# Fused attention stage: transposed scores beside the scores, and maxima subtracted in PSUM by TensorE

## What is computed

```python
def _L1_xattn_ref(query, key, value, ...):
    qn = _layer_norm(query, ln1_g, ln1_b)
    kn = _layer_norm(key, ln1_g, ln1_b)
    vn = _layer_norm(value, ln1_g, ln1_b)
    Q = (qn @ wq + bq).reshape(B, Sq, H, HD)
    K = (kn @ wk + bk).reshape(B, Sk, H, HD)
    V = (vn @ wv + bv).reshape(B, Sk, H, HD)
    scores = jnp.einsum('bqhd,bkhd->bhqk', Q, K) / jnp.sqrt(jnp.float32(HD))
    attn = jax.nn.softmax(scores, axis=-1)
    out = jnp.einsum('bhqk,bkhd->bqhd', attn, V).reshape(B, Sq, E)
    x = residual + out @ wo + bo
    y = _layer_norm(x, ln2_g, ln2_b)
    return x + jax.nn.gelu(y @ w1 + b1, approximate=False) @ w2 + b2
```

## Time and profile of the kernel before

| | |
|---|---|
| median of 3 runs | 1391.83 us (1389.43 to 1393.59) |
| profiled execution, its own time | 1399.14 us |
| span of its trace | 1397.3 us |
| granted TensorE clock, mean | 0.967 of 2.4 GHz |
| busy: TensorE, VectorE, ScalarE, GpSimd | 89%, 68%, 71%, 64% |
| fused stage with its projections | about 916 to 1264 us of the span |
| last feed-forward | about 1264 to 1397 us |

### The profile page before, as it was taken

One profiled execution on the slowest core, in us unless ns is written; L12 is line 12 of the kernel. 1 busy time (PEld: TensorE's weight loads), 2 busy tenths in 40 slices (PEclk: granted clock), 3 DMA queues, 4 the chain that ended last, 5 costly groups with the idle time before them and its releaser, 6 DMA issues. The chain is left out here.

```text
span 1397.3 us, 59862 instructions
## 1 busy us (share of the span) xinstructions
PE 1242.1 (89%) x23050; PEld 1031.0 (74%) x23050; DVE 953.1 (68%) x2152; ACT 988.4 (71%) x1972; POOL 899.7 (64%) x1432
## 2 busy tenths in 40 slices
PE   4999999989999998958999999985878788788997
PEld 2777877777878887837999999953666666665775
DVE  3888888876787886594555555546889999854331
ACT  1778777767888887346787776624988888865553
POOL 2577777776677665216999998767677777413331
PEclk9999999999999999579999999997999999999999
DMA  4233343322222220051222222243222222112221
GB/s 125 77 108 117 110 126 106 114 86 86 83 82 83 82 76 26 16 136 39 69 65 68 66 67 67 66 143 103 63 68 68 73 73 73 41 49 61 68 74 39
DMA packets 137984, 109.81 MB, mean 79 GB/s; under 512 B 16928, under 2 KB 113696, under 8 KB 137888
## 3 DMA queue, kind: packets, MB, share of 16 engines
q1 hardware_dynamic: 129440, 91.22, 22.1%
q0 software_dynamic: 8448, 17.32, 5.2%
HBM read 74.35 MB, written 34.08 MB: 78 GB/s over the span
## 5 line engine op out<-in xcount | busy, mean ns | idle before, releaser
L907 DVE TENSOR_REDUCE at_mx<-at_ps_s 128x16 f32<-128x1024 f32 x128 | 156.0, 1220 | 91.9 <-PE at_ps_s L587 47.2
L813 ACT ACTIVATE at_pt<-at_ps_t 128x1024 f32<-128x1024 f32 x128 | 130.6, 1020 | 55.3 <-PE at_ps_t L608 54.5
L2357 POOL DMA_INDIRECT ex_xg<-x,ex_ti x136 | 146.3, 1076 | 23.5 <-issue 21.9
L806 ACT ACTIVATE at_pr<-at_dd 128x1024 f32<-128x1024 f32 x128 | 135.2, 1056 | 34.7 <-DVE at_dd L915 34.6
L2471 DVE COPY ex_wt<-experts 128x1156 f32 x133 | 102.7, 772 | 80.4 <-DVE ex_y L2477 74.4
L2429 ACT ACTIVATE ex_hg<-ex_ps_h,ex_wt 128x128 f32<-128x128 f32 x544 | 154.6, 374 | 1.2 <-PE ex_ps_y L2388 1.2
L915 DVE TENSOR_TENSOR at_dd<-at_ps_s,at_mx 128x1024 f32<-128x1024 f32 x128 | 153.7, 1202 | 0.1
L2379 PE MATMUL ex_ps_h<-ex_xt,ex_wt 128*128 128x128 f32 x1088 | 146.5, 278 | 1.0 <-ACT ex_xt L2421 0.8
L2016 POOL DMA_INDIRECT l_yg<-rows,l_sl x128 | 125.8, 983 | 31.9 <-issue 29.4
L608 PE MATMUL at_ps_t<-ident,at_pr 128*128 128x128 f32 x1024 | 140.0, 280 | 6.0 <-issue 5.4
L2388 PE MATMUL ex_ps_y<-ex_wt,ex_hg 128*128 128x128 f32 x1088 | 143.6, 275 | 0.4 <-ACT ex_hg L2429 0.4
(11 more groups left out here) (264 smaller groups left out, 3166.5 us busy)
## 6 DMA issues: line engine op xcount, KB each, us to landing
rows<-ex_y SPq DMA_DIRECT2D x136, 64.0 KB
x<-at_ln_out SPq DMA_DIRECT2D x32, 256.0 KB, 3.2
at_kx<-in_xt SPq DMA_DIRECT2D x16, 256.0 KB, 2.8
at_qx<-in_xt SPq DMA_DIRECT2D x16, 256.0 KB, 2.8
at_vin<-in_xt SPq DMA_DIRECT2D x16, 256.0 KB, 2.8
at_xr<-in_x SPq DMA_DIRECT2D x16, 256.0 KB, 3.0
cx<-in_ctx SPq DMA_DIRECT2D x16, 256.0 KB, 3.2
x1t<-at_xt SPq DMA_DIRECT2D x16, 256.0 KB, 3.3
```

Source lines behind the costliest of these rows:

```text
L806: act.activation(pr[:, p], dd[:, p], ACT.Exp, scale=SCALE).then_inc(p_ready, 1)
L813: act.activation(pt[:, 2 * h + p], ps_t[:, :, :, :], ACT.Copy).then_inc(pt_ready, 1)
L907: dve.tensor_reduce(mx[:, p], ps_s[:, :, 4 * p:4 * p + 4, :], AX.X, ALU.max).then_inc(mx_ready, 1)
L2357: pool.indirect_dma_start(out=xg[:, s, :], out_offset=None, in_=x_src, in_offset=bass.IndirectOffsetOnAxis(ap=ti[:, s:s + 1], axis=0)).the ...
```

## The change

Scores are now made in units i = 0 to 3 of a group (half h = i // 2, row-group pair rp = i % 2) of two row groups with all four sequences. `scores(a, i)` makes the unit's products and, in between, the transposed products of the unit before, with K as the moving and Q as the stationary operand exchanged, straight into `ps_t`. VectorE takes the maxima of the untransposed unit and splits each into three parts, of which the upper 16 bits are bf16 numbers (`split`, two subtractions of 128x16). TensorE turns these parts with one bf16 product (`turn_largest`), ScalarE copies them (`copy_largest`), and TensorE subtracts them from the transposed scores by 8 bf16 products into the same PSUM tile (`take_largest`). ScalarE then takes the exponential from PSUM into `pt`. `subtract`, `turn`, `copy_t` and the buffers `dd` and `pr` are gone. K is masked by 8 DMAs a half from SyncE (SBUF to SBUF) instead of by ScalarE; its bias is added when it is projected. The Q mask and the copy of V are split by halves. Half of V is staged in `x3` instead of in `dd` and `pr`, and the last stage uses `pt` for its late buffers. `project_out` waits for one more semaphore (`y_ready`), and the steps of all five engines are written in another order. The diff of the core; the lists of `step` are shown for VectorE and GpSimd:

```diff
+                def mask_k(a, h):
+
+                    if a.unrolled and a.g == 0 and h == 0:
+                        sp.wait_ge(kt_ready, NG)
+                        sp.wait_ge(set_up, 2)
                     if beyond(a.g, 0):
+                        sp.wait_ge(s_ready, 4 * a.g + 2 * h - 1)
+                    for j in range(2):
+                        for r in range(4):
+                            heads = slice(32 * r + 16 * j, 32 * r + 16 * j + 16)
+                            sp.dma_start(kb[heads, h, :, j, :],
+                                         zt[heads, bass.ds(a.place * GT + GT // 2 * h, GT // 2)].rearrange(
+                                             "p (b s) -> p b s", b=QB)).then_inc(in_k[h], 16)
...
+                def scores(a, i):
+
+                    n, h, rp = 4 * a.g + i, i // 2, i % 2
+                    before_h = h if rp == 1 else 1 - h
+                    own, last = a.exists(), i > 0 or a.shift(-1).exists()
+                    if own and rp == 0:
+                        pe.wait_ge(in_k[h], 16 * 8 * (a.g + 1))
+                        pe.wait_ge(qb_ready[h], a.g + 1)
+                    if own and beyond(n, 0):
+                        pe.wait_ge(mx_ready, n)
+                    elif own:
                         pe.wait_ge(kt_ready, NG)
                         pe.wait_ge(vt_ready, NG)
+                    if last and beyond(n, 2):
+                        pe.wait_ge(pt_ready, n - 2)
                     for b in range(QB):
+                        if own:
+                            for r in range(2):
+                                rows = slice(64 * rp + 32 * r, 64 * rp + 32 * r + 32)
+                                mm = pe.matmul(ps_s[:, r, 2 * b:2 * b + 2, :], qb[rows, h, b, :, :], kb[rows, h, b, :, :],
+                                               start=(b == 0), stop=(b == QB - 1), skip_group_check=True)
+                        if last:
+                            for r in range(2):
+                                rows = slice(64 - 64 * rp + 32 * r, 64 - 64 * rp + 32 * r + 32)
+                                mm = pe.matmul(ps_t[:, 1 - rp, r, b, :], kb[rows, before_h, b, :, :],
+                                               qb[rows, before_h, b, :, :], start=(b == 0), stop=False,
+                                               skip_group_check=True)
                     mm.then_inc(s_ready, 1)
+                def turn_largest(a, i):
+
+                    n, rp = 4 * a.g + i, i % 2
+                    pe.wait_ge(parts_ready, n + 1)
+                    if beyond(n, 0):
+                        pe.wait_ge(pt_ready, n)
+                    pe.matmul(ps_t[:, 1 - rp, 0, 0, :], mx[:, rp, :].bitcast(BF16).rearrange("p (x t) -> p x t", t=2)[:, :, 1],
+                              same_b[:, :], start=True, stop=True).then_inc(mt_ready, 1)
+
+                def take_largest(a, i):
+
+                    n, rp = 4 * a.g + i, i % 2
+                    pe.wait_ge(mc_ready, n + 1)
+                    for b in range(QB):
+                        for r in range(2):
+                            rows = slice(64 * rp + 32 * r, 64 * rp + 32 * r + 32)
+                            mm = pe.matmul(ps_t[:, rp, r, b, :], minus[rows, b, :], mt[rows, :], start=False,
+                                           stop=(b == QB - 1), skip_group_check=True)
+                    mm.then_inc(t_ready, 1)
...
+                def exponent(a, i):
+                    n, h, rp = 4 * a.g + i, i // 2, i % 2
+                    if a.unrolled and n == 0:
+                        act.wait_ge(v_out, 16 * NG)
+                    act.wait_ge(t_ready, n + 1)
+                    if beyond(a.g, 0):
+                        act.wait_ge(pv_ready, 2 * a.g + h - 1)
+                    act.activation(pt[:, h, :, 2 * rp:2 * rp + 2, :].rearrange("p b r q -> p r b q"), ps_t[:, rp],
+                                   ACT.Exp, scale=SCALE).then_inc(pt_ready, 1)
+                def copy_largest(a, i):
+                    n, rp = 4 * a.g + i, i % 2
+                    half = slice(64 * rp, 64 * rp + 64)
+                    act.wait_ge(mt_ready, n + 1)
+                    if beyond(n, 1):
+                        act.wait_ge(t_ready, n - 1)
+                    act.activation(mt[half, :], ps_t[half, 1 - rp, 0, 0, :], ACT.Copy).then_inc(mc_ready, 1)
...
+                def maximum(a, i):
+                    n, rp = 4 * a.g + i, i % 2
+                    dve.wait_ge(s_ready, n + 1)
+                    if beyond(n, 1):
+                        dve.wait_ge(mt_ready, n - 1)
+                    dve.tensor_reduce(largest(rp, 0), ps_s[:, :, :, :], AX.X, ALU.max).then_inc(mx_ready, 1)
+                def split(a, i):
+                    n, rp = 4 * a.g + i, i % 2
+                    dve.wait_ge(mx_ready, n + 1)
+                    dve.tensor_tensor(largest(rp, 1), largest(rp, 0), high(rp, 0), ALU.subtract).then_inc(rest_ready, 1)
+                    dve.wait_ge(rest_ready, n + 1)
+                    dve.tensor_tensor(largest(rp, 2), largest(rp, 1), high(rp, 1), ALU.subtract).then_inc(parts_ready, 1)
...
+                    if a.shift(-1).exists():
+                        recip(g * 2 - 2, 0)
                     if a.exists():
-                        subtract(g * 2 + 1, 0)
+                        maximum(a, 0)
+                        split(a, 0)
                     if a.shift(3).exists():
                         weigh_first(a.shift(3))
+                    if a.shift(-1).exists():
+                        normalise(a.shift(-1), 0)
                     if a.exists():
-                        maximum(g * 2 + 1, 1)
+                        maximum(a, 1)
+                        split(a, 1)
+                    if a.shift(-2).exists():
+                        residual(a.shift(-2))
+                    if a.shift(3).exists():
+                        weigh_second(a.shift(3))
                     if a.shift(-1).exists():
                         recip(g * 2 - 1, 1)
-                    if a.shift(3).exists():
-                        weigh_second(a.shift(3))
                     if a.exists():
-                        subtract(g * 2 + 1, 1)
+                        maximum(a, 2)
+                        split(a, 2)
                     if a.shift(3).exists():
                         own_statistics(a.shift(3))
                     if a.shift(-1).exists():
                         normalise(a.shift(-1), 1)
+                    if a.unrolled and -3 <= g < -1:
+                        for e in ((5, 6, 7, 8), (11, 12, 13, 14, 15))[g + 3]:
+                            keep_v(e)
+                    if a.shift(2).exists():
+                        gain_own(a.shift(2))
+                    if a.exists():
+                        maximum(a, 3)
+                        split(a, 3)
                     if a.shift(2).exists():
                         next_statistics(a.shift(2))
                     if a.shift(3).exists() or a.shift(2).exists():
                         front_moments(a.shift(3))
-                    if a.unrolled and -3 <= g < -1:
-                        for e in ((5, 6, 7, 8), (11, 12, 13, 14, 15))[g + 3]:
-                            keep_v(e)
-                    if a.unrolled and g == -1:
-                        dve.wait_ge(v_out, 16 * NG)
-                    if a.shift(1).exists():
-                        maximum(g * 2 + 2, 0)
-                        maximum(g * 2 + 2, 1)
-                        subtract(g * 2 + 2, 0)
-                        subtract(g * 2 + 2, 1)
-                    if a.exists():
-                        recip(g * 2, 0)
-                    if a.shift(3).exists():
-                        gain_own(a.shift(3))
-                    if a.shift(-1).exists():
-                        residual(a.shift(-1))
-                    if a.shift(1).exists():
-                        maximum(g * 2 + 3, 0)
-                    if a.exists():
-                        normalise(a, 0)
...
+                    if a.unrolled and g == 0:
+                        pool.wait_ge(v_out, 16 * NG)
+                    if a.shift(-1).exists():
+                        spread(g * 2 - 2, 0)
                     if a.shift(2).exists() or a.shift(1).exists():
                         front_rstd(a.shift(2))
                     if a.shift(3).exists():
-                        fetch(a.shift(3), 5, 6)
-                        fetch(a.shift(3), 6, 7)
-                        fetch(a.shift(3), 7, 8)
-                    if a.shift(-1).exists():
-                        spread(g * 2 - 2, 0)
+                        fetch(a.shift(3), 5, 8)
                     if a.shift(4).exists():
                         fetch_open(a.shift(4))
                     if a.shift(-1).exists():
                         add_bias(a.shift(-1))
-                    if a.shift(4).exists():
-                        fetch(a.shift(4), 0, 1)
-                        fetch(a.shift(4), 1, 2)
-                        fetch(a.shift(4), 2, 3)
```

(31 more changed lines are left out.)

245 lines of the change are left out of this document (115 added, 130 removed).

## The result

The changed kernel takes **1484.93 us** (median of 4 runs, 1481.51 to 1488.6) beside 1392.28 us of the kernel before: ratio 1.0669, 95% interval 1.0638 to 1.07. That is 93 us more; 1459 was forecast, in a range of 1424 to 1486, so the measured time lies 1 us inside the upper end. The profiled execution took 1488.6 us with a span of 1486.8 us, 89.5 us longer than the span of before. (The two profiled executions stand 4 and 7 us above the medians of their kernels, which is why 89.5 and 93 differ.)

What follows compares the result with a forecast made beforehand. VectorE was taken to set the pace, busy 92 of 100 us, the other engines close behind. Profiled 1399.1 us + 71 for twelve longer steps - 4 outside them = 1466, as a median 1459 us; range 1424 to 1486.

Steps and rivals of the forecast that it cites:

- The ring: Steps 1 to 12: spread, late gathers, `weigh_first`, `values`, `gain_own`, `shift_own`, next spread; 24.0 us a step for 18.07, +71 us.
- The clock: TensorE's pause ahead of `values` drops the clock to half in all twelve steps; `values` takes 3.6 us instead of 2.0.
- Rival 1: Twelve steps: the ring without the clock drop, step 22.4 us, +48 us, 1440 us in all; chance 0.27.
- Outside the twelve steps ... -4 us: Steps 13 to 15 gain 1 us each, the start 1 us; VectorE's set-up 0 to +3 us, last stage 0.
- rival 3: K's DMAs end last as well in the twelve steps: +1.5 us a step, +18 us, 1477 us; chance 0.12.
- K by DMA, cost 0: Sixteen DMAs a step replace ScalarE's K maskings, hidden by the gather wait: cost 0, bound +1.5 us a step.
- late next: K's DMAs in the steps: were the gather wait that hides them gone, they would be the next to come late.
- The small operations on VectorE: Eight new operations on 128x16 a step, 0.2 us each, 1.6 us together, within 0 to 4.3 us.
- Rival 2: Gathers arrive without holding VectorE: step about 17.0 us, -17 us, 1375 us in all; chance 0.09.
- rival 4: Whole kernel: nothing moves, the waits given up and made cancel, 1392 us; chance 0.03.
- The step without the ring, "some 17 us": Steady step if only the engines' work changed and nothing else happened: falls from 18.07 to some 17 us.

Runs made afterwards that it cites:

- gathers_early: Changed kernel with gathers 5 to 7 of a group issued a step earlier, in the same step as its gathers 0 to 4; 1427.59 us.
- weigh_later: Changed kernel with `weigh_first` moved on VectorE behind `normalise` and `residual`, directly ahead of `weigh_second`, gathers still late; 1443.74 us.
- start_order: Changed kernel with VectorE's second group of `keep_v` moved behind the statistics and moments in two steps ahead of the first; 1472.77 us.
- orders: `early_take_start` with `recip` moved ahead of `weigh_second` on VectorE and `copy_v(a,0)` behind the exponent of unit 3 on ScalarE; 1422.05 us.
- k_on_dve: Changed kernel with K masked by products on VectorE instead of by SyncE's sixteen DMAs a step; 1483.89 us.
- early_take_start: Changed kernel with gathers as in `gathers_early`, start as in `start_order`, and `take_largest` of units 0 and 2 ahead of `values`; 1422.11 us.

## Why the prediction was right, and where it was off

- **The ring.** Right, by term and in sum: 24.0 us forecast, 23.99 measured. Spread to first gather 3.1 us (3.18 forecast), three gathers 3.57 (3.57), landing 1.77 (1.57), `weigh_first` and `normalise` 1.5 (1.58), `values` 3.6 (3.6), from its end to the end of `gain_own` 5.2 (5.4), `shift_own` and three gathers 4.9 (5.0). `gathers_early` and `weigh_later`, which open it at two different places, take 59 and 40 us back. That the sum is right to 0.01 us is in part luck: small errors of 0.1 to 0.2 us cancel, and the second path through `values(a,0)`, which I did not look at, happened to end 0.05 us ahead of the ring.
- **The clock.** The mechanism was right (0.50 under `values` in all five steps looked at, 0.86 over 100 us); its size, 1.6 us a step, was too large. Held, it gave 0.8 to 1.05, although `values` did fall to 2.0 us; the other 0.6 us are the wait of the first spread for its reciprocal, by the second path. Rival 1's step of 22.4 us would have been 22.9.
- **"Outside the twelve steps ... -4 us".** This term was mis-sized: measured +18.5 (12.0 ahead, 2 in steps 13 and 14, 4.5 behind the last load). I costed VectorE's set-up and looked no further at the start; the change had also swapped `keep_v` with the front work there, whose price `start_order` gives as 12 us. And I gave steps 13 to 15 a gain of 1 us each for freed engines; steps 13 and 14 lost 1 us each instead (18.1 us beside 17.1). TensorE was not freed there, and `orders` gets 17.2 with `recip` and `copy_v` in other places. The 4.5 us at the end were not tried by themselves; that the last stage costs 0 was nearly right (0.8).
- **The number.** With the ring exact, the term above alone puts the forecast 22.5 us low in the span. That 1484.93 still lies under 1486 is luck: the upper end was placed above rival 3 (1477), whose mechanism did not come, and no term of the range allowed for 18.5 us outside the twelve steps.
- **K by DMA, cost 0.** Right, by the one wait of 0.7 us in 160 and by `k_on_dve`. The pitch was 0.73 us, near the upper of my two ends; "late next" is what `orders` shows.
- **The small operations on VectorE.** 0.2 us each was forecast; 0.17 us alone, 0.2 on average in the changed kernel, up to 1.9 us beside GpSimd's addition in `orders`.
- **Rivals.** Rival 2, gathers that hold nobody, is excluded by the 6.1 us wait of `weigh_first`; rival 3, K's DMAs on the path, by TensorE's single wait for them and by `k_on_dve`; rival 4 by the time.
- **The step without the ring, "some 17 us".** Too low: 20.2 with early gathers (at a clock of 0.95 to 0.97), 19.1 at best. 17.2 is reached only where there is no front work, and the old form takes 17.1 there.

## What to carry to other kernels

When a change reorders hand-written queues, look at what each wait holds up behind it: here a wait for gathers placed ahead of one small multiplication made one loop through all four engines, and the step 5.9 us longer in spite of the work saved. Opening that loop gave back 3.8 of the 5.9: when the largest wait goes, the next path is often close behind, so look for it before you price the repair. Read the unrolled steps at the ends with the same care as the loop; two swapped calls cost 12 us there. And before relieving two engines, ask whether the third, which gets their work, is not the one that sets the pace once the slack is gone.

## What the runs showed of the hardware

A VectorE subtraction of 16 columns, 0.17 us by itself, took 0.89 to 1.41 us beside a 1.3 us GpSimd addition of two SBUF tensors (`early_take_start`), and ended with it. In `orders` one took 1.92 us: it began at 1127.86, 0.6 us ahead of the addition and beside the gather that GpSimd was issuing, and ended with the addition. After the 4.3 us pause the granted clock was 0.50 for 5 us, 0.84 in the microsecond behind them and then 1.00, and it fell again to 0.50 in each of the next four steps. SyncE issued 64-piece copies within SBUF at 0.73 us each.
